# Last layer of a four-layer kernel: the gated products stay in their PSUM bank, and the weights are split in three pieces

## The reference, cut to what matters

```
probs = softmax(flat @ gate_W.T);  top_v, top_i = top_k(probs, 2)
g = silu(flat @ w1_e);  u = flat @ w3_e            # each of 8 experts, 128 -> 512
out_e = (g * u) @ w2_e                             # 512 -> 128
routed = the two chosen experts' out_e, weighted by their gates
shared = the same through 8 small experts of 64 hidden features, mean of the 8
x = x + layernorm(0.5 * shared + 0.5 * routed)
```

## Time and profile before

| | |
|---|---|
| time, median of 3 runs | 1784.54 us (1780.53 to 1786.31) |
| the profiled execution | 1779.97 us, of which the span from first to last instruction is 1777.9 us |
| PE busy over the span | 1479.8 us (83%) |
| DVE, ACT, POOL busy over the span | 1265.8 us (71%), 1022.6 us (58%), 826.4 us (46%) |

### The profile page before, as it was taken

How to read it: one execution, slowest core, us unless ns; L and a number is a source line. 1 busy time by engine, 2 the same in 40 slices (tenths; PEclk the granted TensorE clock), 3 DMA queues, 4 the chain that set the end, 5 groups by cost and what they waited for, 6 DMA issues and landing times. The chain is left out here.

```text
span 1777.9 us, 26868 instructions
## 1 busy us (share of the span) xinstructions
PE 1479.8 (83%) x8751; PEld 862.4 (49%) x8757; DVE 1265.8 (71%) x3276; ACT 1022.6 (58%) x1749; POOL 826.4 (46%) x935
## 2 busy tenths in 40 slices
PE   3788888679999999587769999999995787999980
PEld 1444455334444444333334555555552665777760
DVE  1656768568888886358677888878882574888875
ACT  2454555435666666235536777777775654777762
POOL 1244534555666654425731221222001575688875
PEclk8989989779999999689859999999998798999995
DMA  6800000222222221000434435454420023344414
GB/s 212 290 2 1 1 1 1 62 65 73 74 74 74 74 74 25 17 1 1 106 98 123 123 85 134 125 131 124 93 62 25 16 69 101 113 140 124 137 43 142
DMA packets 97225, 143.77 MB, mean 81 GB/s; under 512 B 31778, under 2 KB 64547, under 8 KB 94512
## 3 DMA queue, kind: packets, MB, share of 16 engines
q1 hardware_dynamic: 92096, 133.59, 26.8%
q0 software_dynamic: 4992, 8.48, 1.4%
HBM read 103.93 MB, written 57.22 MB: 91 GB/s over the span
## 5 line engine op out<-in xcount | busy, mean ns | idle before, releaser
L1259 DVE TENSOR_REDUCE ctx_nm<-ctx_s 128x1 f32<-128x512 f32 x496 | 325.1, 681 | 73.2 <-PE ctx_s L1415 72.0
L1259 DVE TENSOR_REDUCE rope_nm<-rope_s 128x1 f32<-128x128 f32 x496 | 221.1, 478 | 60.8 <-PE rope_s L1418 59.3
L1659 ACT ACTIVATE rope_probs<-rope_st 128x1024 f32<-128x1024 f32 (+1 forms) x256 | 171.2, 702 | 132.6 <-PE rope_st L1762 131.3
L1659 ACT ACTIVATE ctx_probs<-ctx_st 128x1024 f32<-128x1024 f32 x192 | 189.8, 1022 | 69.1 <-PE ctx_st L1762 64.9
L1415 PE MATMUL ctx_s<-att_kst,att_qst 96*128 96x512 f32 x496 | 209.4, 452 | 11.6 <-PEq L120 7.7
L1415 PE MATMUL rope_s<-att_kst,att_qst 96*128 96x128 bf16 x496 | 147.7, 313 | 31.3 <-DMA att_kst<-rope_halves 16.7
L1762 PE MATMUL ctx_st<-att_qst,att_kst 98*128 98x512 f32 x512 | 163.9, 403 | 0.0
L1415 PEld LDWEIGHTS ctx_s<-att_kst,att_qst 96*128 96x128 f32 x496 | 95.8, 193 | 124.9 <-issue 55.4
L1524 POOL TENSOR_SCALAR_AFFINE_SELECT rope_probs<-rope_probs 128x256 f32<-128x256 f32 x256 | 98.3, 411 | 106.9 <-ACT rope_probs L1659 106.6
L1778 PE MATMUL ctx_out<-ctx_probs,att_vaug 128*32 128x512 f32 x768 | 135.1, 604 | 0.0
L3036 DVE TENSOR_TENSOR sw_hl<-sw_hf,sw_hh 128x512 fp32r<-128x512 f32 x124 | 129.5, 1044 | 0.1
(11 more groups left out here) (440 smaller groups left out, 3461.5 us busy)
## 6 DMA issues: line engine op xcount, KB each, us to landing
sw_raw<-in_L_ffn_all SPq DMA_DIRECT2D x24, 768.0 KB, 4.5
sw_xs<-in_pad SPq DMA_DIRECT2D x65, 260.0 KB, 9.4
ctx_halves<-att_qk SPq DMA_DIRECT2D x24, 512.0 KB, 5.8
att_qst<-ctx_contexts SPq DMA_DIRECT2D x32, 384.0 KB
att_kst<-ctx_contexts SPq DMA_DIRECT2D x32, 384.0 KB
rope_halves<-att_qk SPq DMA_DIRECT2D x32, 256.0 KB, 3.4
att_qst<-rope_halves SPq DMA_DIRECT2D x32, 192.0 KB, 3.0
att_kst<-rope_halves SPq DMA_DIRECT2D x32, 192.0 KB, 3.3
```

The source lines that it names most:

```text
L1259: nc.vector.tensor_reduce(nm[:, g, j * T + t:j * T + t + 1], bank("s", b, n)[:, 0:keys], AXX, ALU.max, negate=True).then_inc(s_used, 1)
L1659: nc.scalar.activation(prob(n // GH % 2, n % GH)[:, u * units[0]:u * units[0] + units[u]], st_bank[u][:, 0:units[u]], ACT.Exp, scale=SCALE ...
```

## The change

1. `product` writes `silu * u` back into `u_bank` and no longer into SBUF; the ring `hf` is gone. `high_half` and `low_half` read `u_bank`.
2. ACT makes `high_half(m)` right behind `gated(m)`, and DVE `low_half(m)` behind `product(m)`: both halves are in the product's own step. `token_low` and `fetch` stand between `product(m)` and `low_half(m)` where there is one.
3. PE no longer waits for the product ahead of `g`, and waits for `low_half(m - 2)` ahead of `u`.
4. `wh` and `wl` are made in three pieces of 128 x 512. ACT makes a piece at each of `c == 0, 1, 2`, at the end of the step, and POOL waits for each piece. PE waits for all three, and SP, ahead of a load into a `raw` buffer, for all three pieces that read it.

```
             def up(m):
...
-                    pe.wait_ge(wh_ready, uses[i] + 1)
-                    pe.wait_ge(wl_ready, uses[i] + 1)
+                    pe.wait_ge(wh_ready, 3 * (uses[i] + 1))
+                    pe.wait_ge(wl_ready, 3 * (uses[i] + 1))
...
                 if m >= 2:
                     pe.wait_ge(silu_ready, m - 1)
-                    pe.wait_ge(hf_ready, m - 1)
...
+                if m >= 2:
+                    pe.wait_ge(hl_ready, m - 1)
                 mm3(nc, u_bank[m % 2][:], both(uses[i], 1, c), tokens).then_inc(u_ps, 1)
...
-                nc.scalar.activation(wh[s % WR][:], raw[s % 2][:], ACT.Copy).then_inc(wh_ready, 1)
+                nc.scalar.activation(wh[s % WR][:, k], raw[s % 2][:, k], ACT.Copy).then_inc(wh_ready, 1)
...
-                nc.scalar.activation(hh[m % RING][:], hf[m % 3][:], ACT.Copy).then_inc(hh_ready, 1)
+                nc.scalar.activation(hh[m % RING][:], u_bank[m % 2][:], ACT.Copy).then_inc(hh_ready, 1)
...
                 gated(m)
-                if m >= 1:
-                    high_half(m - 1)
+                high_half(m)
...
-                if c == 0 and i + 1 < N and uses[i + 1] != uses[i]:
-                    cut_high(uses[i + 1])
-            high_half(M - 1)
+                if c < 3 and i + 1 < N and uses[i + 1] != uses[i]:
+                    cut_high(uses[i + 1], c)
...
-                pool.wait_ge(wh_ready, s + 1)
-                nc.gpsimd.tensor_tensor(wl[s % WR][:], raw[s % 2][:], wh[s % WR][:].bitcast(F32), ALU.subtract).then_inc(wl_ready, 1)
+                for k in range(3):
+                    pool.wait_ge(wh_ready, 3 * s + k + 1)
+                    nc.gpsimd.tensor_tensor(wl[s % WR][:, k], raw[s % 2][:, k], wh[s % WR][:, k].bitcast(F32), ALU.subtract).then_inc(wl_ready, 1)
...
-                nc.vector.tensor_tensor(hf[m % 3][:], silu[m % 2][:], u_bank[m % 2][:], ALU.mult).then_inc(hf_ready, 1)
+                nc.vector.tensor_tensor(u_bank[m % 2][:], silu[m % 2][:], u_bank[m % 2][:], ALU.mult).then_inc(hf_ready, 1)
...
-                nc.vector.tensor_tensor(hl[m % RING][:], hf[m % 3][:], hh[m % RING][:].bitcast(F32), ALU.subtract).then_inc(hl_ready, 1)
+                nc.vector.tensor_tensor(hl[m % RING][:], u_bank[m % 2][:], hh[m % RING][:].bitcast(F32), ALU.subtract).then_inc(hl_ready, 1)
...
                 product(m)
...
-                if m >= 1:
-                    low_half(m - 1)
+                if i + 1 < N and c == min(turning(i + 1) + 1, FC - 1):
+                    token_low(i + 1)
+                if c == 3 and i >= 1:
+                    fetch(i - 1)
+                low_half(m)
```

More of the change, by code:

```diff
@@ L2553, in routed_layer @@
         silu = [sb(f"silu{k}", [P, S]) for k in range(2)]
-        hf = [sb(f"hf{k}", [P, S]) for k in range(3)]
         hh, hl = ([sb(f"{n}{k}", [P, S], F32R) for k in range(RING)] for n in ("hh", "hl"))
@@ L2599, in load_weights @@
                 if s >= 2:
-                    sp.wait_ge(wl_ready, s - 1)
+                    sp.wait_ge(wl_ready, 3 * (s - 1))
                 sp.dma_start(raw[s % 2][:], w["all"][expert]).then_inc(w_loaded[s % 2], 16)
@@ L2760, in keep, with cut_high @@
                 nc.scalar.activation(YT[:, b * S:(b + 1) * S], flips[b][:], ACT.Copy).then_inc(yT_ready, 1)
-            def cut_high(s):
+            def cut_high(s, k):
                 act.wait_ge(w_loaded[s % 2], 16 * (s // 2 + 1))
@@ L2823, in _ @@
                 if b == 1:
-                    cut_high(0)
+                    for k in range(3):
+                        cut_high(0, k)
             exponent(0)
@@ L3026, in product @@
                 dve.wait_ge(u_ps, m + 1)
-                if m >= 3:
-                    dve.wait_ge(hh_ready, m - 2)
-                    dve.wait_ge(hl_ready, m - 2)
-                nc.vector.tensor_tensor(hf[m % 3][:], silu[m % 2][:], u_bank[m % 2][:], ALU.mult).then_inc(hf_ready, 1)
+                nc.vector.tensor_tensor(u_bank[m % 2][:], silu[m % 2][:], u_bank[m % 2][:], ALU.mult).then_inc(hf_ready, 1)
             def low_half(m):
@@ L3104, in _ @@
                     plan()
[L3105 to L3109, removed]
             fetch(N - 1)
```

## The result

The changed kernel takes 1843.26 us (median, 1841.89 to 1843.35) against 1782.53 us beside it: 1.034 times the time before, 95% interval 1.031 to 1.036. The forecast was 1853, its range 1820 to 1873.

What follows compares the result with a forecast made beforehand. The prediction took PE to set the pace in routed tiles (busy 96% at the full clock). Profiled 1780.0 + 44 (longer routed tiles) + 26 (clock falls) + 3 (shared tiles' scatter) = 1853 us, range 1820 to 1873.

Steps and rivals of the forecast that it cites:

- The bound and what it removes: Routed tiles: PE sets the pace; its stall behind `xl` goes, at most 0.37 us a tile, 8 us over 22 boundaries.
- ACT's wait for the product: On ACT, `high_half(m)` right behind `silu(m)` waits for DVE's product: 0.97 us more a step, against 0.64 free.
- The round trip of 1.47 us: Time from ACT's `silu` through DVE's product to `hh`, 1.47 us, where before the change it was 0.50.
- The rival in which the wait is hidden: ACT keeps up, PE's stall behind `xl` goes: a tile of 9.4 us, 1774 us in all; chance 0.05.
- The thirds: Weights in three pieces: the last, cut at the end of `c == 2`, comes on the path, +0.75 us a tile.
- The term of 44 us: Routed tiles of 11.8 us, 2.0 more than now, over the 22 boundaries between them: +44 us.
- The clock: TensorE's clock falls behind PE's stall of about 2.4 us in some routed tiles: 15 x 1.75 = +26 us.
- The rival of a holding clock: Nothing falls at a 2.4 us stall: 1827 us, up to 1832 by the median; chance 0.20.
- Two tiles in three: Share of routed tiles in which the clock was taken to fall: 15, at 1.75 us each; ends 0 and 39 us.
- The shared tiles: Tiles ahead of the routed ones: covered by PE's 11.14 us idle, tail losing under 1 us each; only the scatter's delay counts.
- The term of 3 us: Delay of POOL's scatter in the shared tiles, behind which the first routed rows are loaded: +3 us, between 2 and 5.
- What was costed at nothing: PE's wait for `hl(m - 2)` ahead of `u`, and SP's loads, later by some 5 us: no cost.

Runs made afterwards that it cites:

- e9: The changed kernel with the high half made on DVE right behind the product and the weights in one piece at `c == 0`: 1772.85 us.
- e8: The changed kernel with the high half made on DVE, between product and low half, instead of on ACT: 1770.72 us.
- e7: The kernel before with only the order moved (both halves in the product's step, `xl` and `dT` ahead of `hl`), products in SBUF, weights in one piece: 1842.82 us.
- e1: The changed kernel with the weights again in one piece at `c == 0`: 1818.63 us.
- e3: The changed kernel with seven more matmuls of no use on PE at the end of each routed tile, in PE's stall: 1823.17 us.
- e10: e7 with the high half made on DVE, right behind the product; product in SBUF, weights in one piece: 1818.28 us.
- e4: The kernel before with only the products written back to their PSUM bank; halves one step behind, weights in one piece: 1786.13 us.

## Why the prediction was right, and where its sizes were off

*The bound and what it removes.* Right. The stall was `xl` behind a long `hl`; `hl` from PSUM takes 0.69 us beside `wl`. That the cure is worth something shows only where no new wait is put in: e9, in which PE never stalls ahead of `g`, has 205.5 us of routed stretch against 215.6 (its ACT is rid of `hh` too). Its tile is 0.50 us shorter, and e8's 0.63, so "at most 0.37 us a tile" was too little. The row of PE ahead of the earlier trace rows shows most of it:

```profile
1607.65 0.39 PE L110 MATMUL sw_d<-sw_hh,sw_wl 128*128 128x512 f32 x1
```

From this start to that of `g` at 1608.40 pass 0.75 us, where matmuls go every 0.23: the stall of 0.37 us cost 0.52.

*ACT's wait for the product.* Right, and the main cause: e7 and e1 have it without the thirds and lose 58 and 34 us, e8 is without it and gains. e8 frees ACT of `hh`'s own time too, but before the change ACT carried `hh` with 0.64 us a step to spare, so it is the wait that made its list too long. The round trip of 1.47 us was measured as 1.48 and 1.38. The rival in which the wait is hidden turned on 0.97 us more a step against 0.64 free, and that comparison held: ACT's idle time for `g` fell to 24.4 us without going to nothing, as the longer tile has PE's stall in it.

*The thirds.* Right in kind, 0.75 us a tile forecast, 0.35 measured (11.43 against 11.08). The mis-sized part is the chain from `silu` of `c == 2` to the next tile's: 5.41 us (1649.84 to 1655.25) for 5.7. PE starts 0.11 us behind POOL's `wl`, where the row of its start behind DVE's `xl` gave 0.36; the round trip was 0.09 shorter. In `c == 1`, `yo` took 1.00 us of ACT and not 1.1: 3.50 for 3.59. Together a tile of 11.43 us without a fall instead of 11.8. The term of 44 us measured 36.4 (252.0 in e3 less 215.6).

*The clock.* Right that it falls in some tiles and not in others: 12 of 22 at 1.5 us, 18 us, where 15 at 1.75 gave 26. The stall was 2.04 us for 2.4. The rival of a holding clock fell, and e3 shows its number: 1823 against the 1827 given for it. "Two tiles in three" was a choice between two stall lengths that no row decided, so that it came near 12 of 22 is in part luck. The Trainium skill (TensorE: Matmul & The Clock Gate, "HAM oscillation") describes a kernel with waits of some 3 to 5 us, in which the clock returns to its low level for every group of matmuls behind a wait. Here, with stalls of 2 us, it did so behind 12 and not behind 10.

*The shared tiles.* The term of 3 us measured 6.7. The first scatter came 2.1 us later, counted from the layer's first `silu` (1404.33 less 1392.6, 1408.84 less 1395.0), as forecast. The prediction named the second cause, the scatter of step 14 that waits for the product, but gave it no size of its own; it is larger, 3.93 us where the earlier trace rows has 0.30. All of POOL's waits for a product there come to 10.1 us, against 2.3 before, while the 64 scatters themselves take 62.6 us for 65.5; so the last one starts 6.8 us later, counted from the first `silu`. POOL's timeline after, and PE's first routed input, which answers to the earlier trace rows:

```profile
1408.84 1.22 POOL L2876 DMA_INDIRECT sw_xs<-sw_rows,sw_slots  x1 [5.80 <-issue]
...
1460.43 0.96 POOL L2876 DMA_INDIRECT sw_xs<-sw_rows,sw_slots  x1 [3.93 <-DVE sw_u L3027]
...
1499.82 0.96 POOL L2876 DMA_INDIRECT sw_xs<-sw_rows,sw_slots  x1 [0.30 <-issue]
```

```profile
1506.05 1.12 PE L2707 MATMUL sw_t_in<-ident,sw_xin 128*128 128x128 f32 x4 [7.12 <-DMA sw_xin<-sw_xs]
```

The shared tiles themselves lost 11 us and not "less than 1 each"; PE's wait for the first routed rows, 11.14 us before and 7.12 now, covers 4 of them.

*What was costed at nothing.* PE's wait for `hl(m - 2)` ahead of `u` has no row among PE's waits of 1500 to 1730 us in the changed kernel. SP's later loads cost nothing either: ACT has no idle time ahead of a weights piece (0.0 in the group of L2766). The write to PSUM is not dear: 693 ns.

*The sum.* 36.4 + 18.1 + 6.7 + 2.4 + 0.1 = 63.7 us of span, against 44 + 26 + 3 = 73: two terms too large by 8 each, one too small by 4, and 2.4 of the difference that is not the change's.

*The rule on the shared port.* One SBUF input is not always safe beside `wl`. The Trainium skill (SBUF — State Buffer, "Who interferes with whom") exempts a VectorE instruction with at most one SBUF input from contending with GpSimd only outside the modes in which it uses both of its port pairs, and names copies and casts among those that can enter them. e10 agrees: a copy with one input, from SBUF, 0.43 us by itself, was held for all of `wl`, 3.69 us.

## What to carry to other kernels

Before a step is moved behind a result of its own step, add up the round trip through the other engine and compare it with the idle time of the waiting engine per step; if it doesn't fit, give the moved operation to the engine that has the result already. A stall of some 2 us on TensorE may cost its own length and nearly as much again in clock, so its price is read from the trace with the clock's column beside it. An edit that is neutral or a loss alone can be what makes another pay: test pairs, not parts only.

## What the runs showed of the hardware that was not expected

- Stalls of nearly the same length act differently on TensorE's clock: 2.06 us ahead of `g` (1554.95) was followed by 3.4 us at 1.2 GHz, 2.02 us (1567.98) was not. It is not the length that decides: the stall of 2.06 us before the `g` of 1543.53 was followed by none, and that of 2.02 us before the `g` of 1641.27 by one. What decides was not found. In e1 stalls of 1.69 to 1.76 us, one a tile from the fourth routed tile on, left the clock at 1.00 throughout.
- A DVE copy of 128x512 takes 0.43 us from SBUF by itself, 0.69 from PSUM, and 3.69 from SBUF beside POOL's `wl`. The slower source is the safer one here.
- POOL's indirect DMA issues suffer as well when DVE reads two operands from SBUF: in e7 a send that began 0.07 us into an `hl` took 1.46 us, and one that began with DVE idle 0.97. POOL's and DVE's timelines:

```profile
1642.52 0.97 POOL L2886 DMA_INDIRECT sw_ys<-sw_yo,sw_xin  x1 [0.30 <-issue]
1643.80 1.46 POOL L2886 DMA_INDIRECT sw_ys<-sw_yo,sw_xin  x1 [0.30 <-issue]
```

```profile
1643.73 0.68 DVE L3034 TENSOR_TENSOR sw_hl<-sw_hf,sw_hh 128x512 fp32r<-128x512 f32 x1
```

With the product in PSUM the sends take 977 ns on the mean (1146 before), and 978 in e4, where that is the only edit.
